# Four node blocks a loop turn on TensorE, VectorE and ScalarE, TensorE's loop bodies cut at another place, and one activation ahead of the first loop

## The chip, the cores and the metric

The kernel runs on one core of one Trainium2 chip. The metric is the device time of one launch in microseconds (us). Times of single instructions are given in us or ns.

## What is computed

100,000 nodes have 64 features each; 50,000 edges, sorted by destination, give `src` and `dst`. Four graph layers follow one another, and each ends in `x = layernorm(x + layer(x))`:

```
L0: three SAGE layers   h = relu(h @ w_self + (segment_sum(h[src], dst) / deg) @ w_neigh + b)
L1: two GCN layers      out = segment_sum(norm * (x @ W)[s], d) + b      (with self loops)
L2: GIN                 x + relu(relu((x + segment_sum(x[src], dst)) @ W1 + b1) @ W2 + b2)
L3: messages            mlp([x[src], x[dst], edge_attr]) summed by dst, then mlp([x, sum])
```

Everything is float32.

## The kernel before

The nodes are padded and cut into 50 blocks (`NB`) of 2,048 nodes, 16 tiles of 128. The program is a chain of passes over all blocks, with a barrier between passes: `Sage0`, `Sage1`, `Sage2`, `Gcn1`, `Gcn2`, `Gin`, `Messages` (empty in this run) and `Update`. Each pass emits a fast version (`windows=True`, the one that runs for sorted edges) and a general one behind a branch on a flag (`both_ways`, L577).

In each pass:

- **GpSimd** gathers the source rows of the block's edges by indirect DMAs of 128 rows into a ring in SBUF, 8 a block (L628), in `Update` 16 a block (L1665). Its loop takes eight blocks a turn.
- **VectorE** builds 0/1 matrices from the edges' destinations (`one_hots`, L649, two for each block), takes the segment sums out of PSUM, and does most of the element work and of the layer norm.
- **TensorE** does the segment sums (`sums`, L659 and L664): for each tile two matrix products of a 0/1 matrix with a ring slot. Which slot that is stands in the table `slots`, so that TensorE's sequencer first loads the slot numbers into registers (`TENSOR_LOAD`, L659) and computes an address ahead of each product. Between sums stand transposes (L968, L1222), first layers (L1208, L1349, L1801 to L1804) and products (L974, L1227). In `Gcn2` there are also matrix products without a use, `stay_warm` (L766).
- **ScalarE** moves results from PSUM to SBUF with an activation, and does squares, roots and part of the norm.
- **SyncE** issues the loads and stores of the blocks. Its loop takes four blocks a turn.

Every engine has its own program; semaphores, which count uses, order them. The loops of TensorE, VectorE and ScalarE are all made by `bodies` (loop at L586): `by=2` blocks a turn in a hardware loop, 24 turns, and the last two blocks unrolled behind it (VectorE and ScalarE in `Update`: 23 turns and four blocks). A turn ends with a compare-and-branch on the engine's sequencer.

Segment sums run one block ahead: in a body for block m, `collect` makes the sums of block m + 1. Where a body of TensorE begins in each pass, before the change:

- `Sage0`: transposes of chunk 0 of block m (four chunks of four tiles), transposes of chunk 1, first layer of chunk 0, sums of chunk 0 of block m + 1, and so on; it ends with the products of chunk 3. Between the transposes of chunks 0 and 1 ScalarE must have emptied the shared PSUM bank (`evacuate`, L1316).
- `Sage2`, `Gcn1`, `Gcn2`: at the segment sums.
- `Sage1`, `Gin`, `Update`: at transposes.

Of the kernel before, what the change touches and what calls it, by code (L numbers as in the profile page):

```python
# [25 lines left out]
ACT = mybir.ActivationFunctionType  # L26
# [34 lines left out]
def build(nc, z, a, out):  # L61
# [512 lines left out]
    def both_ways(eng, general, windows):  # L574
# [4 lines left out]
        with eng.Else():  # L579
            windows()  # L580

    def bodies(eng, body, by=2, behind=2):


        n = (NB - behind) // by
        with eng.Fori(0, n) as it:  # L586
            for v in range(by):
                body(it * by + v, it * (by // 2) + v // 2, v % 2)
        for m in range(n * by, NB):
            body(m, m // 2, m % 2)  # L590
# [12 lines left out]
    def later(m, i, u):  # L603
        return m + 1, i + u, 1 - u
# [165 lines left out]
    class Pass:  # L770
# [133 lines left out]
        def vector_loop(self, ve, windows):  # L904
            for m in range(self.ahead - 1):
                self.hots(ve, m, m, windows)
            self.take_block(ve, 0, 0, 0, windows)
            self.hots(ve, self.ahead - 1, (self.ahead - 1) % 2, windows)
            bodies(ve, lambda m, i, u: self.vector(ve, m, i, u, windows))

        def scalar_loop(self, act, windows):
            bodies(act, lambda m, i, u: self.scalar(act, m, i, u, windows))

        def tensor_loop(self, pe, windows):
            if windows:
                for q in range(2):
                    self.collect(pe, 0, 0, 0, q)
            bodies(pe, lambda m, i, u: self.tensor(pe, m, i, u, windows))

        def gpsimd_windows(self, pool):  # L920
            gather_pool(pool, self.table, self.W, self.pitch, self.last_sum)
# [55 lines left out]
    class Sage2(Pass):  # L977
# [43 lines left out]
                for q in range(2):  # L1021
                    norm_square(act, m + 1, q, pre_of, adds=True)

        def tensor(self, pe, m, i, u, windows):
            if windows:
                for q in range(2):
                    self.collect(pe, *later(m, i, u), q)
            for q in range(2):
                pe.wait_ge(S(f"out{q}"), now(m))
                pe.wait_ge(S(f"ev{q}"), before(m))  # L1030
                pair_transposes(pe, group(store_a[u], q), ps[2 + q]).then_inc(S(f"tr{q}"), 1)
            for q in range(2):
                pe.wait_ge(S(f"ev{q}"), now(m))
                pe.wait_ge(S(f"y{q}"), before(m))
                pair_products(pe, tp[q], wg1, ps[4 + q]).then_inc(S(f"mm{q}"), 1)


    class Gcn1(Pass):
# [33 lines left out]
        def tensor(self, pe, m, i, u, windows):  # L1072
            if windows:
                self.collect(pe, *later(m, i, u), 0)
            for q in range(2):
                pe.wait_ge(S(f"pre{q}"), now(m))
                pe.wait_ge(S(f"ev{q}"), before(m))
                pair_transposes(pe, tmp[1][q], ps[2 + q]).then_inc(S(f"tr{q}"), 1)
            if windows:
                self.collect(pe, *later(m, i, u), 1)  # L1080
            for q in range(2):
                pe.wait_ge(S(f"ev{q}"), now(m))
                pe.wait_ge(S(f"y{q}"), before(m))
                pair_products(pe, tp[q], wg2, ps[4 + q]).then_inc(S(f"mm{q}"), 1)


    class Gcn2(Pass):
# [41 lines left out]
        def scalar(self, act, m, i, u, windows):  # L1129
# [4 lines left out]
            if exists(m + 1):  # L1134
                for q in range(2):
                    norm_square(act, m + 1, q, self.pre(1 - u), True)

        def tensor(self, pe, m, i, u, windows):
            if windows:
                for q in range(2):  # L1140
                    self.collect(pe, *later(m, i, u), q)
                    stay_warm(pe, m * 2 + q, 9)


    class Gin(Pass):
# [107 lines left out]
    class Sage0(Chunks):  # L1253
# [42 lines left out]
        def vector(self, ve, m, i, u, windows):  # L1296
# [7 lines left out]
            for q in range(2):  # L1304
# [2 lines left out]
                own(2 * q + 1)  # L1307
                self.take(ve, *later(m, i, u), q, windows)

        def scalar(self, act, m, i, u, windows):  # L1310
            A = nc.scalar
            self.stored(act, i, u)

            def evacuate(c):
                act.wait_ge(S(f"tr{c}"), now(m))
                A.activation(load_a[u][D:P, c * 512:(c + 1) * 512], ps[4][D:P, :], ACT.Copy).then_inc(S(f"ev{c}"), 1)  # L1316

            def hidden(c):
                act.wait_ge(S(f"hid{c}"), now(m))
                act.wait_ge(S(f"nmm{(c + 2) % 4}"), now(m) if c >= 2 else before(m))  # L1320
                A.activation(tp[c % 2][:, :], ps[5], ACT.Relu, bias=b0c[:, :]).then_inc(S(f"rel{c}"), 1)  # L1321

            def neighbours(c):
                act.wait_ge(S(f"nmm{c}"), now(m))
                A.activation(store_b[u][:, c * 512:(c + 1) * 512], ps[6], ACT.Copy).then_inc(S(f"n1{c}"), 1)  # L1325

            evacuate(0)
            for c in range(4):
                if c < 3:
                    evacuate(c + 1)  # L1330
                hidden(c)
                if c >= 1:
                    neighbours(c - 1)
            neighbours(3)

        def tensor(self, pe, m, i, u, windows):
            def former(name, c):

                pe.wait_ge(S(f"{name}{(c + 3) % 4}"), now(m) if c else before(m))

            def turn(c):
                pe.wait_ge(S(f"mean{c}"), now(m))
# [8 lines left out]
            def products(c):  # L1351
                pe.wait_ge(S(f"rel{c}"), now(m))
                former("n1", c)
                tile_products(pe, tp[c % 2], w1[:, 0:H], ps[6])
                former("s1", c)
                tile_products(pe, tp[c % 2], w1[:, H:2 * H], ps[7]).then_inc(S(f"nmm{c}"), 1)
# [12 lines left out]
            products(0)  # L1369
            next_sums(1)  # L1370
            turn(3)
            hidden(2)
            products(1)
            next_sums(2)
            hidden(3)
            products(2)
            next_sums(3)
            products(3)


    class Sage1(Chunks):
# [210 lines left out]
    class Update(Pass):  # L1592
# [107 lines left out]
        def vector_loop(self, ve, windows):  # L1700
# [9 lines left out]
            bodies(ve, lambda m, i, u: self.vector(ve, m, i, u, windows), behind=4)  # L1710

        def vector(self, ve, m, i, u, windows):
            V = nc.vector
# [49 lines left out]
        def scalar_loop(self, act, windows):  # L1763
# [4 lines left out]
            bodies(act, lambda m, i, u: self.scalar(act, m, i, u, windows), behind=4)  # L1768

        def scalar(self, act, m, i, u, windows):  # L1770
            self.turned(act, "u", 0, m, windows)
# [55 lines left out]
        def tensor_loop(self, pe, windows):  # L1827
            if windows:
# [9 lines left out]
            bodies(pe, lambda m, i, u: self.tensor(pe, m, i, u, windows))  # L1838

        def tensor(self, pe, m, i, u, windows):  # L1840
            both = windows and exists(m + 2)
# [154 lines left out]
```

## Time and profile before

| | |
|---|---|
| time, median of 3 runs | 6260.33 us (6242.03 to 6272.64) |
| profiled execution: span from first to last instruction | 6282.3 us; no other time of that execution is recorded |
| busy share of the span | TensorE 88%, weight loads 79%, VectorE 66%, GpSimd 62%, ScalarE 36% |
| mean granted TensorE clock | 0.897 of full speed |
| pass, us from the span's start | `Sage0` 131 to 1317, `Sage1` 1350 to 2031, `Sage2` 2052 to 2803, `Gcn1` 2833 to 3475, `Gcn2` 3494 to 4147, `Gin` 4182 to 4985, `Update` 5040 to 6282 |

In the profile PE is TensorE's matrix product, PEld its weight load (it overlaps with PE), DVE VectorE, ACT ScalarE, POOL GpSimd, SP SyncE; a q behind the name is the engine's sequencer. Register, branch and semaphore instructions are not counted as busy. PEclk is the granted clock of TensorE, 1.00 being 2.4 GHz and 0.50 being 1.2 GHz; a value between them is the mean over a stretch that has both. An idle time is put down to what released the engine; "issue" means that nothing the profile shows was waited for. A row of windows has, in this order: stretch in us, its length, busy us of PE, PEld, DVE, ACT and POOL with the number of instructions (x), granted clock, share of the DMA engines, GB/s.

### The profile page before, as it was taken

How to read it: one execution, taken by the hardware profiler on the slowest of the kernel's cores; microseconds unless marked ns; L12 is line 12 of the kernel's file. 1: busy time of each engine (PE TensorE's matmuls, PEld its weight loads, DVE VectorE, ACT ScalarE, POOL GpSimd, SP SyncE). 2: the span in 40 equal slices, each digit the busy share in tenths (PEclk: the TensorE clock that was granted, in tenths of full speed). 3: DMA queues.
4: the chain of work that ended last, by engine and by line, in shares of the span. 5: the costliest groups of instructions: out<-in, count | busy, mean ns of one | idle time of the engine just before them, and what ended most of it. 6: DMA issues, size and time to landing. Idle time of an engine off the chain costs nothing. (4 is left out here: it accounts for less than half of the span.)

```text
span 6282.3 us, 130219 instructions
## 1 busy us (share of the span) xinstructions
PE 5525.7 (88%) x39618; PEld 4963.8 (79%) x39619; DVE 4169.7 (66%) x6902; ACT 2249.6 (36%) x6826; POOL 3865.2 (62%) x3226
## 2 busy tenths in 40 slices
PE   3888898969998888978999899969999689999998
PEld 3777777759998788878999899967777567777776
DVE  4444444447776789885666788858888746665655
ACT  0333333322222333330001588843333234444443
POOL 3442442337885666637777677856666377777773
PEclk9999999989999778778888899978888899999998
DMA  1333333335555455543334344432222222222222
GB/s 34 127 121 118 129 112 126 112 123 201 200 201 177 136 161 157 158 142 92 101 101 107 119 141 141 147 80 80 83 85 84 63 58 75 71 71 71 70 72 53
DMA packets 259156, 706.87 MB, mean 113 GB/s; under 512 B 86436, under 2 KB 87620, under 8 KB 236646
## 3 DMA queue, kind: packets, MB, share of 16 engines
q1 hardware_dynamic: 156198, 586.53, 26.5%
q0 software_dynamic: 102848, 119.09, 10.0%
q8 instruction: 43, 0.70, 0.0%
q14 instruction: 67, 0.55, 0.0%
HBM read 389.05 MB, written 314.60 MB: 112 GB/s over the span
## 5 line engine op out<-in xcount | busy, mean ns | idle before, releaser
L664 PE MATMUL ps_all<-arena 128*128 x22400 | 2944.7, 295 | 438.6 <-issue 357.4
L664 PEld LDWEIGHTS ps_all<-arena 128*128 128x128 f32 x22400 | 2871.2, 211 | 548.9 <-issue 543.9
L649 DVE TENSOR_TENSOR arena<-iota,window 128x2048 f32<-128x2048 f32 x708 | 1599.0, 2283 | 30.3 <-issue 24.9
L628 POOL DMA_INDIRECT arena<-n_t,ix_now x800 | 980.4, 1225 | 566.7 <-issue 283.5
L628 POOL DMA_INDIRECT arena<-y_t,ix_now x800 | 996.1, 1245 | 353.9 <-issue 248.3
L628 POOL DMA_INDIRECT arena<-x_rows,ix_now x400 | 453.3, 1133 | 674.1 <-DMA ix_now<-src_ix 413.1
L628 POOL DMA_INDIRECT arena<-x_t,ix_now x400 | 493.5, 1234 | 326.3 <-DMA ix_now<-src_ix 177.1
L1665 POOL DMA_INDIRECT store_a<-x_t,ix_now x400 | 476.5, 1191 | 201.0 <-issue 124.7
L1227 PEld LDWEIGHTS ps_all<-w,tp 128*128 128x128 f32 x4000 | 492.7, 196 | 86.4 <-issue 85.6
L1301 DVE TENSOR_TENSOR store_a<-ps_all,b1r 128x512 f32<-128x512 f32 x200 | 138.3, 692 | 626.3 <-PE ps_all L1227 626.3
L1665 POOL DMA_INDIRECT store_a<-x_t,ix_dst x400 | 450.4, 1126 | 136.8 <-issue 136.5
L1227 PE MATMUL ps_all<-w,tp 128*128 128x128 f32 x4000 | 500.9, 279 | 1.3 <-ACT store_b L1325 0.8
L1403 DVE SCALAR_TENSOR_TENSOR tmp<-ps_all,invdeg,load_a 128x128 f32<-128x128 f32 x800 | 225.2, 344 | 166.5 <-PE ps_all L664 118.5
L1719 DVE TENSOR_TENSOR tmp<-ps_all,bu2r 128x256 f32<-128x256 f32 x200 | 84.9, 425 | 335.5 <-PE ps_all L1227 335.5
L1070 ACT ACTIVATE tp<-ps_all,bg1c 128x512 f32<-128x512 f32 x100 | 65.0, 685 | 595.3 <-PE ps_all L968 594.3
L719 ACT ACTIVATE sq<-tmp 128x64 f32<-128x64 f32 x800 | 191.7, 241 | 229.7 <-DVE tmp L704 229.7
L730 ACT ACTIVATE stat<-stat,eps_c 128x8 f32<-128x8 f32 x400 | 107.7, 293 | 424.3 <-DVE stat L744 424.0
L974 PE MATMUL ps_all<-wg,tp 128*128 128x128 f32 x1600 | 243.0, 315 | 3.4 <-ACT tp L1019 1.1
L1430 ACT ACTIVATE store_b<-ps_all 128x256 f32<-128x256 f32 x200 | 71.7, 384 | 483.4 <-DVE store_a L1416 483.4
L1804 PE MATMUL ps_all<-tp,wu 128*128 128x512 f32 x400 | 213.9, 617 | 33.7 <-ACT tp L1748 33.7
L1227 PEld LDWEIGHTS ps_all<-wu,tq 128*128 128x128 f32 x1600 | 202.5, 192 | 51.7 <-issue 47.8
L1349 PE MATMUL ps_all<-load_a,w 128*128 128x512 f32 x400 | 239.5, 684 | 0.3 <-ACT tp L1321 0.3
(185 smaller groups left out, 7778.5 us busy)
## 6 DMA issues: line engine op xcount, KB each, us to landing
x_t<-store_a SPq DMA_DIRECT2D x150, 512.0 KB, 3.1
load_b<-x_t SPq DMA_DIRECT2D x150, 512.0 KB, 3.3
s_t<-store_a SPq DMA_DIRECT2D x50, 1024.0 KB
n_t<-store_b SPq DMA_DIRECT2D x50, 1024.0 KB
load_a<-s_t SPq DMA_DIRECT2D x50, 1024.0 KB
y_t<-store_b SPq DMA_DIRECT2D x100, 512.0 KB
load_a<-x_cols SPq DMA_DIRECT2D x50, 512.0 KB
s_t<-store_a SPq DMA_DIRECT2D x50, 512.0 KB
```

Source lines behind the costliest of these rows:

```text
L628: pool.indirect_dma_start(out=slot_rows(at, W, pitch), out_offset=None, in_=table, in_offset=bass.IndirectOffsetOnAxis(ap=ix_now[:, at:at ...
L649: V.tensor_tensor(hot_matrices(at, q), iota[:, :].unsqueeze(1).unsqueeze(1).to_broadcast([P, 2, GT, P]), window[:, :, bass.ds(m * NT + q * ...
L664: last = pe.matmul(out(j), hot_matrices(at, j // GT)[:, k, j % GT, :], ring[:, bass.ds(places[k][j - first] * W, W)], start=(k == 0), stop ...
L719: last = A.activation(sq[q][:, j * D:(j + 1) * D], tmp[0][q][:, j * D:(j + 1) * D], ACT.Square, accum_out=stat[:, q, 2, j:j + 1])
L730: nc.scalar.activation(stat[:, q, 3, :], stat[:, q, 2, :], ACT.Sqrt, bias=eps_c[:, :], scale=1.0 / D).then_inc(S(f"sd{q}"), 1)
L974: last = pe.matmul(bank[:, r * P:(r + 1) * P], lhs[:, r * P:(r + 1) * P], w[:, :], start=True, stop=True)
L1227: last = pe.matmul(bank[:, r * P:(r + 1) * P], lhs[:, r * P:(r + 1) * P], w, start=True, stop=True)
L1301: V.tensor_tensor(tiles3(store_a[u][:, c * 512:(c + 1) * 512], H), tiles3(ps[7], H), row(b1r, H, CT), ALU.add).then_inc(S(f"s1{c}"), 1)
L1349: pe.matmul(ps[5], w0[:, :], load_a[u][:, c * 512:(c + 1) * 512], start=True, stop=True).then_inc(S(f"hid{c}"), 1)
L1403: last = nc.vector.scalar_tensor_tensor(tmp[c % 2][q][:, r * P:(r + 1) * P], agg[:, r * P:(r + 1) * P], invdeg[:, bass.ds(m * NT + c * CT ...
L1665: pool.indirect_dma_start(out=self.pairs(u, h)[:, to:to + D], out_offset=None, in_=x3_t, in_offset=bass.IndirectOffsetOnAxis(ap=ix[:, at:a ...
L1804: pe.matmul(ps[4 + s], wu1[:, :], tp[s][:, :], start=True, stop=True).then_inc(S(f"uhid{s}"), 1)
```

## The change

1. `bodies` gets `by=TURN`, four, in the fast version of TensorE, VectorE and ScalarE in all passes: 12 turns and two unrolled blocks in place of 24 and two (VectorE and ScalarE in `Update`: 11 turns and six blocks in place of 23 and four). The general version keeps two.
2. TensorE's body is cut in two: `tensor(m)` is the latter part for block m and then calls `front(m + 1)`, the first part of the next block; one `front(0)` stands ahead of the loop. The order of the instructions on TensorE stays as it was; only where the loop's branch stands in it is new. Bodies now begin: `Sage0` at the products of chunk 3, `Sage2` at the transposes behind both sums, `Gcn1` at the products, `Gcn2` at `stay_warm`. `Sage1`, `Gin` and `Update` have no `front`.
3. `Sage0.scalar_loop` does one Relu on a single element for each partition ahead of the loop.

```diff
+    TURN = 4
-            bodies(ve, lambda m, i, u: self.vector(ve, m, i, u, windows))
+            bodies(ve, lambda m, i, u: self.vector(ve, m, i, u, windows), by=TURN if windows else 2)
-            bodies(act, lambda m, i, u: self.scalar(act, m, i, u, windows))
+            bodies(act, lambda m, i, u: self.scalar(act, m, i, u, windows), by=TURN if windows else 2)
+        def front(self, pe, m, i, u, windows):
+            pass
-            bodies(pe, lambda m, i, u: self.tensor(pe, m, i, u, windows))
+            self.front(pe, 0, 0, 0, windows)
+            bodies(pe, lambda m, i, u: self.tensor(pe, m, i, u, windows), by=TURN if windows else 2)
 # Sage2
-        def tensor(self, pe, m, i, u, windows):
+        def front(self, pe, m, i, u, windows):
             if windows:
                 for q in range(2):
                     self.collect(pe, *later(m, i, u), q)
+
+        def tensor(self, pe, m, i, u, windows):
...
+            self.front(pe, *later(m, i, u), windows)
 # Gcn2
+        def front(self, pe, m, i, u, windows):
+            if windows:
+                self.collect(pe, *later(m, i, u), 0)
+
         def tensor(self, pe, m, i, u, windows):
             if windows:
-                for q in range(2):
-                    self.collect(pe, *later(m, i, u), q)
-                    stay_warm(pe, m * 2 + q, 9)
+                stay_warm(pe, m * 2, 9)
+                self.collect(pe, *later(m, i, u), 1)
+                stay_warm(pe, m * 2 + 1, 9)
+            self.front(pe, *later(m, i, u), windows)
 # Sage0
+        def scalar_loop(self, act, windows):
+
+            nc.scalar.activation(stat[:, 1, 4, 0:1], eps_c[:, :], ACT.Relu)
+            super().scalar_loop(act, windows)
...
         def tensor(self, pe, m, i, u, windows):
+            self.products(pe, m, 3)
+            self.front(pe, *later(m, i, u), windows)
```

`Sage0.front` holds what `Sage0.tensor` held, without the products of chunk 3; `Gcn1.front` holds sums, transposes and sums, and `Gcn1.tensor` the products and the next `front`. `Update`, which has loops of its own, gets the same `by`.

## Rows read from the trace of the kernel before

**Rows 1.** The page's first part: busy us, share of the span, instructions.

```profile
PE 5525.7 (88%) x39618; PEld 4963.8 (79%) x39619; DVE 4169.7 (66%) x6902; ACT 2249.6 (36%) x6826; POOL 3865.2 (62%) x3226
```

**Rows 2.** Busy time by windows, one for each of six passes.

```profile
131.00:1317.00 1186.00, 1057.95 (x7536) 911.60 (x7536) 518.86 (x1085) 404.27 (x622) 433.95 (x381) 0.94 0.37 119
1350.00:2031.00 681.00, 652.53 (x5600) 635.90 (x5600) 508.08 (x1099) 172.04 (x400) 516.75 (x400) 0.98 0.57 191
2052.00:2803.00 751.00, 672.85 (x4376) 644.77 (x4376) 660.55 (x992) 270.76 (x1777) 453.98 (x393) 0.78 0.50 152
2833.00:3475.00 642.00, 596.85 (x4400) 591.61 (x4400) 401.76 (x398) 64.95 (x100) 485.81 (x393) 0.83 0.35 101
4182.00:4985.00 803.00, 722.13 (x4600) 611.15 (x4600) 668.41 (x998) 278.92 (x500) 483.87 (x392) 0.86 0.27 80
5040.00:6282.00 1242.00, 1160.37 (x7568) 925.91 (x7568) 718.90 (x1194) 493.24 (x896) 897.96 (x773) 0.98 0.24 67
```

**Rows 3.** Waits of POOL in the passes Gcn1 and Update.

```profile
POOL arena L628 <- issue: 118.6, 368, 4.2
...
POOL store_a L1665 <- issue: 253.2, 764, 3.5
```

**Rows 4.** One line's instructions: ScalarE's L1316, whole span.

```profile
L1316 ACT ACT_TABLE_LOAD  x24: 1283/1283/1283, 101.8 to 1232.9; - x24
```

**Rows 5.** Timeline of ACT and PE around the end of a turn of Sage0.

```profile
1138.29 1.28 ACT L1316 ACT_TABLE_LOAD   x1
...
1140.32 0.63 PE L1222 MATMUL ps_all<-ident,load_b 128*128 128x128 f32 x4 [2.25 <-ACT load_a L1316]
...
1143.18 1.99 PE L664 MATMUL ps_all<-arena 128*128 x16 [1.38 <-issue]
...
1162.48 0.63 PE L1222 MATMUL ps_all<-ident,load_b 128*128 128x128 f32 x4 [0.96 <-ACT load_a L1316]
```

**Rows 6.** Windows from block to block of Sage0, columns as in rows 2.

```profile
1140.30:1162.50 22.20, 19.85 (x153) 17.40 (x153) 9.46 (x19) 7.51 (x12) 2.84 (x4) 1.00 0.32 108
1162.50:1187.50 25.00, 21.48 (x153) 18.45 (x153) 11.61 (x27) 8.79 (x13) 0.00 (x0) 0.93 0.33 122
...
1235.20:1260.90 25.70, 24.43 (x153) 20.66 (x152) 9.43 (x18) 7.51 (x12) 0.00 (x0) 0.80 0.23 78
```

**Rows 7.** Windows of two turns of Sage2, columns as in rows 2.

```profile
2157.50:2184.20 26.70, 21.54 (x179) 20.02 (x178) 26.70 (x41) 10.94 (x72) 21.21 (x19) 1.00 0.58 179
2184.20:2216.10 31.90, 29.01 (x178) 27.80 (x178) 26.78 (x41) 11.01 (x72) 17.25 (x17) 0.73 0.46 148
```

**Rows 8.** Timeline of PE in Sage2: segment sums that open a turn.

```profile
2160.83 7.46 PE L664 MATMUL ps_all<-arena 128*128 x64 [1.96 <-issue]
...
2307.84 11.52 PE L664 MATMUL ps_all<-arena 128*128 x64 [2.07 <-issue]
```

**Rows 9.** Sequencer instructions of three lines: ns minimum/median/maximum.

```profile
L586 PEldq COMPARE_BRANCH  x168: 76/208/250, 179.8 to 6224.7; - x168
...
L659 PEldq TENSOR_LOAD <-slots x1800: 328/588/1862, 118.3 to 6233.4; - x180
...
L577 PEldq COMPARE_BRANCH  x9: 235/438/3658, 94.0 to 4995.8; - x9
```

**Rows 10.** The chain of work in Update: a sum in each block.

```profile
5100.48 3.78 PE ps_all L664 x32
5124.14 3.78 PE ps_all L664 x32
...
5148.32 3.78 PE ps_all L664 x32
```

**Rows 11.** A whole turn of Sage0, by windows, columns as in rows 2.

```profile
1135.50:1182.70 47.20, 41.35 (x307) 35.85 (x306) 21.07 (x45) 16.30 (x25) 7.03 (x6) 0.96 0.34 118
```

**Rows 12.** DMA queues from 300 to 1200 us: every queue that moved a packet.

```profile
q1 hardware_dynamic: 15416, 99.72, 31.7%
q0 software_dynamic: 9312, 9.55, 5.2%
```

More of the change, by code:

```diff
@@ L1070, in scalar @@
                 nc.scalar.activation(tp[q][:, :], ps[2 + q], ACT.Relu, bias=bg1c[:, :]).then_inc(S(f"ev{q}"), 1)
-        def tensor(self, pe, m, i, u, windows):
+        def front(self, pe, m, i, u, windows):
+            if not exists(m):
+                return
             if windows:
@@ L1080, in tensor @@
                 self.collect(pe, *later(m, i, u), 1)
+        def tensor(self, pe, m, i, u, windows):
             for q in range(2):
@@ L1136, in scalar, with front @@
                     norm_square(act, m + 1, q, self.pre(1 - u), True)
+        def front(self, pe, m, i, u, windows):
+            if windows:
+                self.collect(pe, *later(m, i, u), 0)
         def tensor(self, pe, m, i, u, windows):
             if windows:
-                for q in range(2):
-                    self.collect(pe, *later(m, i, u), q)
-                    stay_warm(pe, m * 2 + q, 9)
+                stay_warm(pe, m * 2, 9)
+                self.collect(pe, *later(m, i, u), 1)
+                stay_warm(pe, m * 2 + 1, 9)
+            self.front(pe, *later(m, i, u), windows)
     class Gin(Pass):
@@ L1334, in scalar, with products, former, front @@
             neighbours(3)
-        def tensor(self, pe, m, i, u, windows):
+        def products(self, pe, m, c):
+            def former(name):
+                pe.wait_ge(S(f"{name}{(c + 3) % 4}"), now(m) if c else before(m))
+            pe.wait_ge(S(f"rel{c}"), now(m))
+            former("n1")
+            tile_products(pe, tp[c % 2], w1[:, 0:H], ps[6])
+            former("s1")
+            tile_products(pe, tp[c % 2], w1[:, H:2 * H], ps[7]).then_inc(S(f"nmm{c}"), 1)
+        def tensor(self, pe, m, i, u, windows):
+            self.products(pe, m, 3)
+            self.front(pe, *later(m, i, u), windows)
+        def front(self, pe, m, i, u, windows):
+            if not exists(m):
+                return
             def former(name, c):
@@ L1349, in hidden @@
                 pe.matmul(ps[5], w0[:, :], load_a[u][:, c * 512:(c + 1) * 512], start=True, stop=True).then_inc(S(f"hid{c}"), 1)
[L1351 to L1356, printed above, removed]
             def next_sums(c):
@@ L1368, in tensor @@
             hidden(1)
-            products(0)
+            self.products(pe, m, 0)
             next_sums(1)
@@ L1372, in tensor @@
             hidden(2)
-            products(1)
+            self.products(pe, m, 1)
             next_sums(2)
             hidden(3)
-            products(2)
+            self.products(pe, m, 2)
             next_sums(3)
-            products(3)
     class Sage1(Chunks):
@@ L1709, in vector_loop @@
             self.messages(ve, 0, windows)
-            bodies(ve, lambda m, i, u: self.vector(ve, m, i, u, windows), behind=4)
+            bodies(ve, lambda m, i, u: self.vector(ve, m, i, u, windows), by=TURN if windows else 2, behind=4)
         def vector(self, ve, m, i, u, windows):
@@ L1767, in scalar_loop @@
             self.message_units(act, 0, windows)
-            bodies(act, lambda m, i, u: self.scalar(act, m, i, u, windows), behind=4)
+            bodies(act, lambda m, i, u: self.scalar(act, m, i, u, windows), by=TURN if windows else 2, behind=4)
         def scalar(self, act, m, i, u, windows):
@@ L1837, in tensor_loop @@
                     self.collect(pe, 0, 0, 0, q)
-            bodies(pe, lambda m, i, u: self.tensor(pe, m, i, u, windows))
+            bodies(pe, lambda m, i, u: self.tensor(pe, m, i, u, windows), by=TURN if windows else 2)
         def tensor(self, pe, m, i, u, windows):
```

## The prediction

> **What bounds the kernel now.** I read the busy shares first [rows 1]: TensorE is busy in 88% of the span, no other engine in more than 66%. Since the passes are parted by barriers, the share says little; the windows by pass say which engine sets the pace in each [rows 2].
>
> `Sage0`: TensorE (1058 of 1186 us), GpSimd far from it. `Sage1`: TensorE is busy 652.5 of 681 us at a clock of 0.98, so there is almost no idle time for a better loop to win. `Sage2`: VectorE is busy 660.6 of 751 us and TensorE 672.9, but at a clock of 0.78; the two take turns. `Gcn1`: TensorE works at 0.83 and GpSimd is the bound: 485.8 us of gathers plus 118.6 us of idle time, 0.32 us ahead of each, is 604 of 642 us [rows 2, 3]. `Gcn2` is alike. `Gin`: TensorE 722 of 803 us at 0.86. `Update`: the chain of waits runs mostly over TensorE [rows 10], with GpSimd just beneath: 898.0 + 253.2 = 1151 of 1242 us [rows 2, 3].
>
> So there are two kinds of time that a change of TensorE's loops can reach: idle time at a turn's end, and the half-speed clock that follows idle time.
>
> **The table load of `Sage0`.** ScalarE has 24 table loads of 1.283 us, one in each turn, all on the first activation of the loop body [rows 4]; ScalarE's work needs none, since the other blocks do the same activations without one. TensorE waits for that activation: 2.25 us at the turn's end, against 0.96 us in the block between two ends [rows 5]. The difference of 1.29 us is the load, and nothing covers it. The first load, at 101.8 us, lies ahead of the first gather and stays in another form: the new Relu brings it, at the same place. The new Relu makes the table's state known ahead of the loop, so I take it that the 23 others go: 23 x 1.29 = 30 us. Were the load to stay in the loop, twelve turns in place of 24 would still give half, 15 us.
>
> The Trainium skill (ScalarE: Activation LUTs, What ACT_TABLE_LOAD costs) gives the load 1283 ns, and another 1380 ns for a drain, for each switch to another set. The trace agrees on the first and shows no second part in TensorE's wait; by the page the sum would be 23 x 2.66 = 61 us.
>
> **The clock in `Sage0`.** A block that holds no table load and no slow stretch takes 22.2 us; one with a table load and a clock of 0.93 takes 25.0, so that 25.0 - 22.2 - 1.3 = 1.5 us are the clock's; a block whose clock is 0.80 takes 25.7, which is 3.5 us for the clock [rows 6]. The pass's mean is 1186 / 50 = 23.7 us a block, so the clock costs 23.7 - 22.2 - 0.6 (half a table load) = 0.9 us a block, some 45 us in all. A clock falls behind both kinds of idle time: the one with the table load, and the shorter pair, 0.96 us and then some 1.4 us for the slot numbers ahead of the sums [rows 5, 6]. The longer idle time goes, the shorter pair stays in each block. If every block then had a slow stretch at 1.5 us, that is 50 x 1.5 = 75 us, 30 worse than now, and the table's gain is gone; if none had, 45 us are won. The rows decide for neither; the nearest is that the cost remains as it is, and I take 0, bounds -45 and +30.
>
> **The turn's end itself.** On TensorE's sequencer the branch takes 0.208 us [rows 9], and two register instructions beside it some 0.08 more, about 0.29 us. VectorE's and ScalarE's branches I cost at nothing: both wait for TensorE around them in the passes that TensorE sets, and if that cover were gone, as in a `Sage2` that VectorE bounds, they would be below the 0.29 us of TensorE's. Where TensorE's body begins at the sums, these 0.29 us stand in a row with the slot loads (0.588 us each, up to 1.862 [rows 9]) between the last product and the first sum. That row of steps is 1.96 to 2.07 us of idle time in `Sage2` [rows 8]. Behind the change the branch stands behind 64 sum products, where the sequencer is ahead, and the gap is 0.29 us shorter. The slot loads are not moved against the products: their stall stays, in every block.
>
> Directly that is 24 x 0.29 = 7 us at most. But a turn without a slow stretch takes 26.7 us, with VectorE busy in all of them, and one with it 31.9 at a clock of 0.73; the same 64 sum products take 7.46 and 11.52 us [rows 7, 8]. All 50 blocks at 13.35 us would be 668 us, 83 less than now. Half of the turn ends go and the others are hidden, so fewer slow stretches should begin; but idle times of 1.7 us remain, and 1.96 us was harmless once while 2.07 was not. Bounds: 0 and 83. I take a quarter, 20 us, nearer to the nothing that an idle time only a seventh shorter suggests.
>
> **`Gcn1`, `Gcn2`, `Sage1`.** In the first two GpSimd's gathers set the pace; a faster turn only makes TensorE wait longer for rows. Only what follows the last gather could gain. `Sage1`'s end lies beneath products. I take 0, bounds 0 and 15 us for the tails.
>
> **`Gin`, `Update`.** Their bodies begin where they did; 12 turn ends fewer are 12 x 0.29 = 3.5 us in `Gin`, taken as 4, with its slow stretches (clock 0.86) as they are. In `Update` the same sum in neighbouring blocks is 23.66 and then 24.18 us apart [rows 10]: 0.52 us for a turn's end, so 12 x 0.52 = 6 us, if GpSimd allows it (it has 91 us of slack).
>
> **The sum.** 30 + 0 + 20 + 0 + 4 + 6 = 60 us, from 6282.3 us to 6222.3 us for the profiled execution. Its span lies 22 us above the median of the runs; against the median: 6260 - 60 = 6200 us.
>
> **The rivals.**
>
> *The clock takes the gain back.* TensorE gets faster by little, and waits at the same places. In `Sage0` the pair of idle times that stays meets a slow stretch in every block (+30), so nothing of 30 is left; `Sage2` keeps its pattern. For it: the block of 25.0 us at 0.93 begins behind the shorter pair [rows 5, 6]. Against it: the longest slow stretch, at 0.80, follows the table load. Left are 4 + 6 us: 6250 us.
>
> *The clock stays up.* `Sage0` wins 30 + 45 us, `Sage2` 50 of its 83, `Gin` and the tails 15, with 6 in `Update`: 146 us, so 6114 us. For it: the turn at 26.7 us exists [rows 7]. Against it: it is rare, and the slot loads stay.
>
> *Slower: a turn of four blocks no longer fits where the sequencer keeps its code.* Now it fits: in 900 us of `Sage0` no packet moved on any queue but the two for data [rows 12], and the branch at L586 never took over 0.250 us. A turn of `Sage0` has 307 + 306 products and weight loads [rows 11] and the sequencer's own on top; four blocks double it, more than any loop of the trace shows. Where a target is not at hand, the trace has the price: the branch at L577 took up to 3.658 us, against 0.235 [rows 9], so 3.4 us. In the two longest loops, `Sage0` and `Update`, with 12 turns each, and with a slow stretch of 3.5 us behind each such stop [rows 6], that is 24 x 6.9 = 166 us; with the 60 won, 6260 + 106 = 6366 us. It decides as soon as a turn is larger than the store; against it stands only that nothing near the limit shows at half the size.
>
> The Trainium skill (Runtime: NRT & Kernel Launch, Instruction fetch mechanics) says that a taken branch whose target lies outside the pages held forces a fetch, and that TensorE holds 2,048 instructions, the other engines 512. By that size a turn of four would fit and this rival would fall; by its remark that a store is only two lines it could bite. No run here shows the limit.
>
> *The change does only part of what it says*: the table load stays in the loop. Then 15 + 20 + 10 = 45 less 10 for more slow stretches: 6225 us.
>
> **How the numbers follow.** Forecast 0.49, the clock takes it back 0.22, the clock stays up 0.18, slower 0.07, table load stays 0.04. Half a per cent is 31 us and about what a measurement of this kernel can tell from no change, so the bound for faster is 6229 us. The forecast falls below it nine times in ten, the clock staying up always, the remaining table load half the time, the second case rarely: 0.49 x 0.9 + 0.18 + 0.02 + 0.03 = 0.67. Slower is the code rival and a little: 0.08. The rest, 0.25, is no change. The range goes from the case of the clock staying up, 6110, to a little above the case in which it takes all back, 6270. The forecast's own range is 6165 to 6235.
>
> **What would show it.** Right: one table load on ScalarE in all of `Sage0`, or none in its loop; TensorE's wait for L1316 at 0.96 us in every block; 84 branches at L586 on TensorE in place of 168; idle time before the sums of `Sage2` at 1.7 us and its clock above 0.78; `Gcn1` and `Gcn2` as long as they were, GpSimd's gathers unbroken; sums in `Update` 23.7 us apart in three of four blocks. Wrong: table loads in each turn; branches at L586 of over 3 us, or instruction packets in the middle of a pass; a clock in `Sage0` below 0.94 with blocks of 23.7 us or more; `Gcn1` shorter by more than 15 us, which would mean that GpSimd was not its bound. The prediction fails upward if slow stretches simply settle elsewhere, and downward if they vanish.

## The result, and the profile after

The changed kernel takes 6173.82 us (median of 4 runs, 6155.04 to 6188.64), the kernel before 6263.97 (4 runs). The ratio is 0.9871, with a 95% interval from 0.9839 to 0.9902. Forecast were 6200 us, 60 less than before; it became 90 less by the medians, and 110 in the profiled executions, from 6282.3 to 6172.2 us of span. Some 20 of those 110 come from the profiled execution of the kernel before, whose span alone lies 18 us above that kernel's median. The mean granted clock rose from 0.897 to 0.914.

The page's first part, as [rows 1]:

```profile
PE 5428.5 (88%) x39618; PEld 4877.7 (79%) x39619; DVE 4168.7 (68%) x6902; ACT 2218.5 (36%) x6804; POOL 3886.7 (63%) x3226
```

TensorE's instructions are the same in number, and it is busy for 97 us less: that is the clock. ScalarE has 22 instructions fewer: 23 table loads are gone and the new Relu has come. The one load left in `Sage0` stands at 101.4 us, on that Relu.

The windows that follow go from the branch that opens a pass to the next one, so that none of a pass's time is left out (those of [rows 2] begin and end inside the pass). Columns: PE, PEld, DVE, ACT and POOL busy, clock, DMA share, GB/s. The kernel before, in the order `Sage0`, `Sage1`, `Sage2`, `Gcn1`, `Gcn2`, `Gin`, and `Update` last:

```profile
101.00:1342.00 1241.00, 1071.10 (x7600) 924.57 (x7600) 542.27 (x1109) 408.31 (x626) 453.34 (x400) 0.93 0.36 117
...
2036.00:2817.00 781.00, 678.43 (x4400) 649.83 (x4400) 672.64 (x1002) 274.78 (x1800) 463.60 (x400) 0.77 0.49 152
...
4163.00:4989.00 826.00, 722.13 (x4600) 611.15 (x4600) 677.30 (x1002) 278.92 (x500) 493.54 (x400) 0.85 0.27 80
```

The changed kernel, the same windows:

```profile
101.00:1288.00 1187.00, 1034.48 (x7600) 898.60 (x7600) 542.50 (x1109) 378.99 (x604) 456.27 (x400) 0.96 0.38 122
1288.00:1979.00 691.00, 646.34 (x5600) 632.03 (x5600) 512.34 (x1100) 170.78 (x400) 513.57 (x400) 0.98 0.58 190
1979.00:2728.00 749.00, 639.51 (x4400) 608.30 (x4400) 673.15 (x1003) 274.42 (x1800) 477.90 (x400) 0.82 0.51 158
2728.00:3382.00 654.00, 589.60 (x4400) 585.20 (x4400) 410.82 (x402) 64.83 (x100) 493.48 (x400) 0.83 0.35 101
3382.00:4072.00 690.00, 615.25 (x5000) 607.22 (x5000) 566.77 (x902) 554.85 (x2500) 509.76 (x400) 0.90 0.43 134
4072.00:4882.00 810.00, 709.13 (x4600) 599.76 (x4600) 677.05 (x1002) 280.06 (x500) 495.85 (x400) 0.86 0.28 81
...
4889.00:6172.00 1283.00, 1169.12 (x7600) 929.88 (x7600) 730.33 (x1202) 494.52 (x900) 925.06 (x800) 0.96 0.24 67
```

`Sage0` is 54 us shorter, `Sage2` 32 and `Gin` 16. The four others (694, 659, 687 and 1286 us before, in the same windows) moved by 5 us or less.

What TensorE waited for in `Sage0` (total us, times, longest), first before, then after:

```profile
PE ps_all L1222 <- ACT load_a L1316: 77.4, 50, 2.2
PE ps_all L664 <- issue: 49.4, 42, 1.4
```

```profile
PE ps_all L666 <- issue: 61.3, 48, 1.4
PE ps_all L1241 <- ACT load_a L1340: 47.7, 50, 1.0
```

The wait for the activation is 29.7 us shorter: 50 waits of at most 1.0 us, where 24 had been 2.2. The wait ahead of the segment sums, which no engine ends ("issue"), grew by 11.9 us. TensorE's busy time fell by 36.6, with the clock up from 0.93 to 0.96. The three make the 54 us: 29.7 - 11.9 + 36.6 = 54.4.

TensorE in a block of `Sage0` after, to be held against [rows 5]:

```profile
1136.34 0.63 PE L1241 MATMUL ps_all<-ident,load_b 128*128 128x128 f32 x4 [0.96 <-ACT load_a L1340]
1136.80 1.02 PE L1391 MATMUL ps_all<-load_a,w 128*128 128x512 f32 x2
1139.03 1.99 PE L666 MATMUL ps_all<-arena 128*128 x16 [1.20 <-issue]
...
1158.33 0.63 PE L1241 MATMUL ps_all<-ident,load_b 128*128 128x128 f32 x4 [0.96 <-ACT load_a L1340]
```

The 2.25 us at a turn's end are gone; the pair of 0.96 us and some 1.2 us for the slot numbers stands in every block. The block takes 22.0 us.

The loop's instructions on TensorE's sequencer (ns minimum/median/maximum), as in [rows 9]:

```profile
L588 PEldq COMPARE_BRANCH  x84: 76/208/247, 240.1 to 6118.5; - x84
...
L661 PEldq TENSOR_LOAD <-slots x1800: 325/588/2137, 118.1 to 6127.6; - x180
```

Half the branches, none longer than before: a turn of four fits. The queues from 300 to 1000 us in the middle of `Sage0`, as in [rows 12], move no instructions:

```profile
q1 hardware_dynamic: 12272, 79.30, 32.7%
q0 software_dynamic: 7939, 8.15, 5.8%
```

### The profile page after: what moved, and what is told of

The parts are those of the page before. It is cut to its first block and busy times, and to the rows that moved or that the text cites. A ratio compares the mean times of both kernels' runs of the same rounds, so it can differ in the third digit from the quotient of the medians.

```text
span 6172.2 us, 129380 instructions
## 1 busy us (share of the span) xinstructions
PE 5428.5 (88%) x39618; PEld 4877.7 (79%) x39619; DVE 4168.7 (68%) x6902; ACT 2218.5 (36%) x6804; POOL 3886.7 (63%) x3226
## 5 line engine op out<-in xcount | busy, mean ns | idle before, releaser
L666 PE MATMUL ps_all<-arena 128*128 x22400 | 2877.2, 291 | 439.2 <-issue 357.8
L666 PEld LDWEIGHTS ps_all<-arena 128*128 128x128 f32 x22400 | 2806.0, 207 | 538.9 <-issue 533.1
L1699 POOL DMA_INDIRECT store_a<-x_t,ix_now x400 | 461.4, 1153 | 201.7 <-issue 124.7
L1699 POOL DMA_INDIRECT store_a<-x_t,ix_dst x400 | 463.7, 1159 | 137.2 <-issue 136.6
L1838 PE MATMUL ps_all<-tp,wu 128*128 128x512 f32 x400 | 212.9, 614 | 29.0 <-ACT tp L1782 29.0
L980 PEld LDWEIGHTS ps_all<-wg,tp 128*128 128x128 f32 x1600 | 223.4, 223 | 16.8 <-ACT tp L1025 16.2
```

Of the source, the lines that this page charges most:

```text
L666: last = pe.matmul(out(j), hot_matrices(at, j // GT)[:, k, j % GT, :], ring[:, bass.ds(places[k][j - first] * W, W)], start=(k == 0), stop ...
L980: last = pe.matmul(bank[:, r * P:(r + 1) * P], lhs[:, r * P:(r + 1) * P], w[:, :], start=True, stop=True)
L1699: pool.indirect_dma_start(out=self.pairs(u, h)[:, to:to + D], out_offset=None, in_=x3_t, in_offset=bass.IndirectOffsetOnAxis(ap=ix[:, at:a ...
L1838: pe.matmul(ps[4 + s], wu1[:, :], tp[s][:, :], start=True, stop=True).then_inc(S(f"uhid{s}"), 1)
```

## The experiments

### The change taken apart

Four kernels on one chip: the Relu alone, all without the Relu, the cut alone, and four blocks a turn alone.

```diff
 e1_table_only: the kernel before, and in Sage0
+        def scalar_loop(self, act, windows):
+            nc.scalar.activation(stat[:, 1, 4, 0:1], eps_c[:, :], ACT.Relu)
+            super().scalar_loop(act, windows)
 e2_all_but_table: the changed kernel without these three lines
 e3_cut_only: e2 with
-    TURN = 4
+    TURN = 2
 e4_four_only: the kernel before with TURN = 4, and in each of the three loops of Pass and of Update
-            bodies(pe, lambda m, i, u: self.tensor(pe, m, i, u, windows))
+            bodies(pe, lambda m, i, u: self.tensor(pe, m, i, u, windows), by=TURN if windows else 2)
```

> The kernel before with the Relu ahead of Sage0's loop and nothing else. If the table load costs only its own time, the 23 loads in the loop go, TensorE's wait for the evacuation is 0.96 us in every block, and Sage0 is 30 us shorter, the other passes as before: 0.995 of the kernel before. If removing the long idle time also spares slow clock, as the changed kernel's Sage0 suggests (54 us shorter in the profile), Sage0 is 45 to 55 us shorter with half the low-clock time: 0.991 to 0.993. If the clock settles elsewhere, Sage0 is about as long as before.

> The changed kernel without the Relu: one table load a turn, so 12 in Sage0's loop. Theory 1 (the load and the clock behind it): Sage0 wins about half, 25 us against the kernel before, the other passes as in the changed kernel, 0.991 to 0.993 of the kernel before. Rival (the gain in Sage0 comes from fewer turn ends and the cut, not from the table): Sage0 is as short as in the changed kernel, near 1187 us from its branch to the next pass's.

> Bodies cut as in the changed kernel, still two blocks a turn, no Relu. If hiding the branch behind work is what helps Sage2, its 2.0 us of idle time ahead of the sums at a turn's end become 1.7, its low-clock time falls from 361 us and the pass is 15 to 35 us shorter; Gin and Update, which are not cut, stay as before; 0.995 to 0.998 in all. If the number of turn ends is what counts, Sage2 stays at 781 us.

> Four blocks a turn, bodies not cut, no Relu. 12 table loads fewer give 15 us in Sage0 (25 with the clock). If the number of turn ends counts in Sage2, half of its slow stretches go: 15 to 35 us; Gin 4 to 16 us shorter, Update 3 to 6; in all 0.990 to 0.995. If the cut is what helps Sage2, that pass stays near 781 us and the whole is at 0.994 to 0.997.

| kernel | median us | ratio to before, 95% | `Sage0` | `Sage2` | `Gin` |
|---|---|---|---|---|---|
| before | 6255.61 | | 1241 | 781 | 826 |
| e1_table_only | 6207.08 | 0.9932 (0.9908 to 0.9957) | 1195 | 777 | 813 |
| e2_all_but_table | 6191.65 | 0.9891 (0.9852 to 0.9930) | 1212 | 760 | 804 |
| e3_cut_only | 6231.47 | 0.9963 (0.9941 to 0.9985) | 1241 | 744 | 825 |
| e4_four_only | 6208.21 | 0.9921 (0.9897 to 0.9945) | 1215 | 755 | 806 |

(The passes are those of each kernel's profiled execution, in us; the median of the kernel before is that of its 21 runs beside these.) `Sage0` in e1, e3 and e4, by windows:

```profile
101.00:1296.00 1195.00, 1041.10 (x7600) 902.97 (x7600) 542.04 (x1109) 378.87 (x604) 452.75 (x400) 0.96 0.38 121
```

```profile
101.00:1342.00 1241.00, 1072.44 (x7600) 925.14 (x7600) 542.22 (x1109) 408.17 (x626) 450.66 (x400) 0.93 0.36 117
```

```profile
101.00:1316.00 1215.00, 1055.41 (x7600) 913.21 (x7600) 542.39 (x1109) 392.91 (x614) 452.06 (x400) 0.94 0.37 119
```

The Relu alone takes 46 us off `Sage0`, not 30. TensorE's wait for the activation falls by the 29.7 us again (77.4 to 47.7), and its busy time by 30.0, 1071.1 to 1041.1: the clock is up from 0.93 to 0.96 with nothing else of this pass changed. With twelve of the 24 loads left, e4 has half of both: the wait is 61.9 us, busy time 15.7 less. The cut alone, which leaves the 24 loads, changes nothing in `Sage0`. So each table load in the loop cost 1.29 us of wait and about as much again in half-speed products behind it. Of the 60 us that both come to for all 23 loads, the wait for the slot numbers takes back some 14. Of the two theories put down ahead of e1 the second held (45 to 55 us were forecast, 46 came). e2, which differs from the changed kernel by the Relu alone, has 12 loads in place of one and takes 1212 us: the rival that fewer turn ends made `Sage0` shorter forecast 1187 and is out.

In `Sage2` both halves of the change work, and don't add: the cut gives 37 us, four blocks a turn 26, the two together 32 in the changed kernel and 21 in e2, which has the same `Sage2`. Two executions of one code thus lie 11 us apart, and the order of the four is not shown; that each is shorter than the 781 and 777 of the uncut loop with two blocks is. In `Gin`, whose code the Relu and the cut don't touch, the three kernels with two blocks took 826, 813 and 825 us; with four a turn it took 810, 804, 806, and 806 and 799 in e6 and e7 below. That is about 16 us for four blocks a turn, with up to 13 us between two executions of the same code.

### How large may a turn be

```diff
-    TURN = 4
+    TURN = 8
```

> The changed kernel with eight blocks a turn (the unrolled rest grows to two blocks on TensorE, ten in Update on VectorE and ScalarE). A turn on TensorE is then some 1,800 to 2,000 sequencer instructions in Sage2, Gcn1, Gcn2 and Gin, some 2,300 in Sage1 and some 3,000 in Sage0 and Update. If there is a limit to the code that is held and it lies between, branches at the loop's line take some 3.5 us in the passes above it, instruction packets move in the middle of these passes, Sage0 and Update are 6 x 7 = 40 us longer each, and the passes below the limit are as in the changed kernel or 5 us shorter: 1.00 of the kernel before. If code streams in ahead of the sequencer at no cost, nothing stops and the whole is at 0.985 to 0.988 of the kernel before, as the changed kernel or a little faster.

Measured: 6292.48 us, ratio 1.0053 (1.0030 to 1.0076). The sequencer's branch, whole span:

```profile
L588 PEldq COMPARE_BRANCH  x42: 76/3652/6967, 333.1 to 6219.4; - x42
```

The median of all branches is 3.652 us in place of 0.208, and in the middle of `Sage0` two more queues now move packets:

```profile
q8 instruction: 51, 0.84, 0.5%
q14 instruction: 20, 0.16, 0.1%
```

Each pass now has five stops. By windows `Sage0` is 20 us longer than with four blocks a turn, `Sage1` 17, `Sage2` 14, `Gin` 33 and `Update` 32; `Gcn1` and `Gcn2` are not longer. For `Sage0` and `Update` 40 each had been forecast. The slower rival was a true mechanism, and four blocks stayed below its edge. To find the edge, six blocks a turn, in one run:

```diff
-    TURN = 4
+    TURN = 6
```

> The changed kernel with six blocks a turn: some 2,200 sequencer instructions in a turn of TensorE in Sage0 and Update, 1,700 in Sage1, 1,350 to 1,480 in the four others. If what is held lies between the 1,490 of the changed kernel's Sage0 and 1,700, the branch takes some 3.5 us in Sage0, Sage1 and Update and 0.2 us elsewhere; if it lies between 1,700 and 2,200, Sage1 is free of it too. If four blocks were already near the edge and other things than size decide, the four shorter passes stop as well.

Measured: 6239.44 us. The branch in `Sage0`, in `Sage1`, in the four passes behind it, and in `Update`:

```profile
L588 PEldq COMPARE_BRANCH  x8: 83/5202/5597, 289.6 to 1285.6; - x8
...
L588 PEldq COMPARE_BRANCH  x8: 76/208/234, 1438.5 to 1987.3; - x8
...
L588 PEldq COMPARE_BRANCH  x32: 76/208/228, 2144.4 to 4883.7; - x32
...
L588 PEldq COMPARE_BRANCH  x8: 76/3332/3777, 5142.9 to 6180.1; - x8
```

Only the two longest bodies stop. From branch to branch the trace records, with the sequencer's own instructions, some 2,213 on TensorE in a turn of six blocks of `Sage0` and 1,705 in one of `Sage1`, which runs on without a stop. At eight blocks a turn of `Sage2` or `Gcn1` has some 1,791, and every branch back stops, for 3.472 and 3.824 us in the median. So the edge lies between 1,705 and 1,791 recorded instructions, and a turn of four in `Sage0`, 1,477, is 13% below the longest turn that ran free. (A trace can lack some records, so that the true numbers may be a little higher.) The price: `Sage0` took 1228 us, 41 more than at four, with seven stops of 5.2 us, and `Update` 1310, 27 more, with seven of 3.3. A stop thus cost 4 to 6 us in all, of which the branch itself is 3.3 to 5.2. The prediction's 6.9 us a stop was too high.

The Trainium skill (Runtime: NRT & Kernel Launch, Instruction fetch mechanics) puts TensorE's store at 2,048 instructions. The runs confirm that a branch back stops the engine once the loop is too long, and that instructions are then fetched in the middle of a pass. They don't show a loop that makes full use of the 2,048. Its remark on two lines, which the prediction weighed, did not bite: the loop of 1,705 ran free.

### Is it the clock, or the wait behind the products

Two theories of what was left in `Sage2` at 749 us, where VectorE's work is 673: the half-speed clock holds TensorE back, or the wait for the slot numbers does, by where it stands. Two kernels from the changed one. The first adds work that computes nothing, nine small products ahead of the sums of each block, to keep TensorE busy. Each is two on TensorE, so that the pass has 900 more:

```diff
 e6_warm_sage2, Sage2.tensor
+            if windows:
+                stay_warm(pe, m, 9)
             self.front(pe, *later(m, i, u), windows)
```

The second reads the slot numbers of the first half's sums at the body's start, ahead of the transposes, and not behind the products. No load is added or taken away (1800 in either kernel):

```diff
 e7_slots_ahead_sage2
+    def places_of(m, tiles):
+        first, n = tiles[0], len(tiles)
+        return [nc.values_load_multi_w_load_instructions(slots[0:1, k, bass.ds(m * NT + first, n)], ...)[1] for k in range(2)]
-    def sums(pe, m, tiles, out, W, at):
+    def sums(pe, m, tiles, out, W, at, places=None):
+        places = places or places_of(m, tiles)
...
         def tensor(self, pe, m, i, u, windows):
+            places = places_of(m + 2, range(GT)) if windows and exists(m + 2) else None
...
-            self.front(pe, *later(m, i, u), windows)
+            self.front(pe, *later(m, i, u), windows, places)
```

> The changed kernel with nine products without a use ahead of the segment sums of each block of Sage2 (2.0 us more work for TensorE a block, 100 us in the pass). They give the sequencer time to load the slot numbers, so that no idle time stands ahead of the sums. If the low clock that follows this idle time is what makes Sage2 longer than VectorE's 13.35 us a block, the pass gets shorter in spite of the added work: from 749 us to 700 to 720, with less than 120 us of low clock (now 274). If TensorE's amount of work is what counts, the pass grows, by up to 50 us. Other passes as in the changed kernel.

> The changed kernel; in Sage2 the slot numbers of the first half of a block's sums are loaded at the beginning of the body, ahead of the transposes, and no longer between products and sums. The idle time ahead of the sums should vanish (1.7 us), and since VectorE takes 13.35 us a block in any case, it moves ahead of the transposes. If any idle time of that size lowers the clock, the pass stays at 740 to 750 us with 270 us of low clock. If it is the place ahead of the sums that matters, because the 64 sum products then run at the low clock while the transposes' idle time is harmless, the pass falls to 700 to 725 us.

`Sage2` by windows, in e6 and in e7:

```profile
1977.00:2711.00 734.00, 672.53 (x5300) 647.00 (x5300) 673.15 (x1002) 272.34 (x1800) 482.65 (x400) 0.91 0.52 161
```

```profile
1977.00:2684.00 707.00, 595.36 (x4400) 571.12 (x4400) 671.79 (x1002) 274.88 (x1800) 485.76 (x400) 0.85 0.55 167
```

e6 lifted the clock from 0.82 to 0.91 and won 15 us of the pass, less than was expected of it (700 to 720 us, and under 120 us of low clock, where a mean of 0.91 over 734 us makes some 130); the kernel's median, 6171.94, cannot be told from the changed kernel's. The added products take 109 us, and TensorE's own work in the pass fell from 640 to 564 (672.5 - 108.7), so the better clock was paid for with more than it gave. e7 lifted the clock only to 0.85 and won 42 us: 6127.65 us, ratio 0.9796 (0.9762 to 0.9831). TensorE's waits in the whole pass, after the change and then in e7:

```profile
PE ps_all L666 <- issue: 63.0, 34, 25.0
PE ps_all L974 <- DVE store_a L760: 42.8, 37, 8.2
```

```profile
PE ps_all L979 <- DVE store_a L765: 84.6, 48, 6.8
PE ps_all L671 <- issue: 25.3, 2, 25.0
```

25 us of "issue" in either are the pass's first wait. The rest of it, 38 us in 33 waits, is gone, but the waits for VectorE grew by 42: TensorE idles as long as before, some 110 us. What fell is its busy time, 639.5 to 595.4 us, and that is the pass's 42 us. The sums alone (busy us of PE and PEld, then clock, DMA share and GB/s), after the change and in e7:

```profile
1979.00:2728.00 749.00, 444.30 (x3200) 437.31 (x3200) 0.82 0.51 158
```

```profile
1977.00:2684.00 707.00, 378.26 (x3200) 377.76 (x3200) 0.85 0.55 167
```

They lost 66 us of busy time, while the transposes and products ahead of them gained 28. So the half-speed clock was the cost, and the place of the idle time decides what runs at it: ahead of the sums it was the 64 sum products of a block, ahead of the transposes it is mostly the few products behind these. That is the second theory put down for e7 (700 to 725 us), but for its word "harmless". Now TensorE waits for VectorE in nearly every block, and VectorE sets the pace, busy 672 of 707 us.

### The same in `Sage0` and `Gin`

e8 does this in three passes: in `Gin` both halves' slot numbers ahead of the transposes, in `Sage0` those of chunk 0 ahead of the last products.

```diff
 e8_slots_ahead_three: e7, and
 Sage0
         def tensor(self, pe, m, i, u, windows):
+            places = places_of(m + 2, range(CT)) if windows and exists(m + 2) else None
             self.products(pe, m, 3)
-            self.front(pe, *later(m, i, u), windows)
+            self.front(pe, *later(m, i, u), windows, places)
...
 Gin
         def tensor(self, pe, m, i, u, windows):
+            places = [places_of(m + 1, range(q * GT, q * GT + GT)) if windows and exists(m + 1) else None for q in range(2)]
...
-                    self.collect(pe, *later(m, i, u), q)
+                    self.collect(pe, *later(m, i, u), q, places[q])
```

> The changed kernel with slot numbers loaded at the beginning of the body in three passes: Sage2 as in the run before (707 us), Gin (both halves of the sums, ahead of the transposes) and Sage0 (chunk 0 of the next block, ahead of the products of chunk 3). If the idle time ahead of the sums and the clock behind it are the cost there too, Sage0 falls from 1187 to 1110 to 1135 us (1.3 us a block and its 88 us of low clock), Gin from 806 to 730 to 780, and the whole is at 0.960 to 0.970 of the kernel before. If Gin and Sage0 wait for other things anyway (VectorE's input to the transposes, ScalarE's evacuation), the idle time moves there and the whole is at 0.977 to 0.981.

Measured: 5934.96 us (4 runs, 5931.63 to 5952.33), ratio 0.9502 (0.9479 to 0.9525). It beats both kernels, lies 239 us below the changed one, and below the range that was forecast for it (0.960 to 0.970): `Sage0`, 1080 us where 1110 to 1135 were expected, makes about half of that. `Sage0`, `Sage2` and `Gin` by windows:

```profile
101.00:1181.00 1080.00, 988.77 (x7600) 880.49 (x7600) 542.00 (x1109) 379.00 (x604) 473.88 (x400) 0.99 0.42 134
...
1864.00:2571.00 707.00, 595.93 (x4400) 571.69 (x4400) 671.82 (x1002) 274.93 (x1800) 485.11 (x400) 0.85 0.54 167
...
3905.00:4637.00 732.00, 633.50 (x4600) 543.30 (x4600) 675.20 (x1002) 277.46 (x500) 505.57 (x400) 0.94 0.31 90
```

`Sage0` lost 107 us more. A stretch of it, with the same instructions as shown above of the changed kernel:

```profile
608.73 0.63 PE L1248 MATMUL ps_all<-ident,load_b 128*128 128x128 f32 x4 [0.96 <-ACT load_a L1347]
609.20 1.02 PE L1399 MATMUL ps_all<-load_a,w 128*128 128x512 f32 x2
610.06 1.90 PE L671 MATMUL ps_all<-arena 128*128 x16
...
629.26 0.63 PE L1248 MATMUL ps_all<-ident,load_b 128*128 128x128 f32 x4 [0.96 <-ACT load_a L1347]
```

No idle time ahead of the sums; the block takes 20.5 us. The 61.3 us of waits are gone, and 45.7 us of busy time with them. Most of that is the clock, now 0.99. Some 12 us are not: in blocks at full clock TensorE is busy for 19.83 us after the change and for 19.54 to 19.61 in e8, as its products follow each other without a break. The wait for the activation alone, 0.96 us, stays in each of the 50 blocks and does little to the clock. The pair did.

In `Gin`, as in `Sage2`, the idle time moves. Its waits (us, times, longest), after the change and in e8:

```profile
PE ps_all L666 <- issue: 95.6, 89, 39.4
PE ps_all L974 <- DVE load_a L1175: 10.5, 27, 1.0
```

```profile
PE ps_all L979 <- DVE load_a L1181: 49.0, 40, 1.5
PE ps_all L671 <- issue: 39.3, 1, 39.3
PE ps_all L979 <- issue: 9.9, 9, 1.5
PE ps_all L1234 <- ACT tp L1206: 4.8, 20, 0.3
```

TensorE idles about as long as before (106 us and 103), in fewer waits (116 and 70). The timeline shows where, first after the change, ahead of either half's sums, then in e8, ahead of the transposes alone:

```profile
4316.50 3.78 PE L666 MATMUL ps_all<-arena 128*128 x32 [0.77 <-issue]
4320.88 5.12 PE L666 MATMUL ps_all<-arena 128*128 x32 [0.59 <-issue]
```

```profile
4315.09 1.25 PE L979 MATMUL ps_all<-ident,load_a 128*128 128x128 f32 x8 [0.99 <-DVE load_a L1181]
...
4320.22 7.26 PE L671 MATMUL ps_all<-arena 128*128 x64
```

The clock is 0.94 in place of 0.86, and busy time falls from 709 to 634 us, which is nearly all of the pass's 78 us. Some 15 of these 76 are not the clock: at full clock the 64 sum products take 7.26 us in one run and twice 3.78 in two.

Last, whether the larger turn is still worth having with the slot numbers ahead:

```diff
 e10_slots_two_a_turn: e8 with
-    TURN = 4
+    TURN = 2
```

> The kernel of the run before last (slot numbers loaded early in Sage0, Sage2 and Gin, bodies cut, Relu ahead) with two blocks a turn in place of four. If the number of turn ends has a cost of its own, the 12 turns more cost 3 to 16 us in Gin and 3 to 6 in Update, and the whole is at 0.952 to 0.956 of the kernel before. If turn ends only mattered through the idle time that they lengthened, ahead of slot loads that are now hidden, the three passes are within 5 us of those with four blocks a turn, and the whole is at 0.949 to 0.952.

Measured: 5974.75 us, ratio 0.9552 (0.9529 to 0.9574), 40 us above e8. In `Sage0` and `Sage2` nothing is lost (1079 and 707 us). `Gin` takes 752 us in place of 732, `Gcn1` 658 in place of 650, `Sage1` 691 in place of 683. Of the two theories neither holds for all: with the slot numbers ahead a turn's end is free in `Sage0` and `Sage2`, and `Gin` is 20 us longer, more than the 3 to 16 of the first theory. The 40 us of the medians are clear of the noise, but by passes only `Gin`'s 20 us are more than executions of one code lie apart: `Gcn1` took 658 to 661 us in the four kernels with two blocks a turn and 650 to 661 in those with four, `Sage1` 688 to 694 and 683 to 691. `Update`, for which the first theory forecast 3 to 6 us, took 1285 and 1288.

## Why the prediction was right, and where its sizes were off

- *The table load.* Right in place and size: 29.7 us of TensorE's wait against 30 in the sum, and 23 loads gone. Nothing of a second part beside the 1.283 us is seen in TensorE's wait: it fell by 29.7 us in e1, too, not by the 61 that come of the figures of the Trainium skill (ScalarE: Activation LUTs, What ACT_TABLE_LOAD costs). What a load cost beyond that is TensorE's clock.
- *The clock in `Sage0`*, "the nearest is that the cost remains as it is, and I take 0". This step was mis-sized: the busy time fell by 36.6 us, the slot waits grew by 11.9, so the term is -24 (the bounds were -45 and +30). The prediction read two kinds of idle time, and weighed the shorter pair against the longer wait by the slow stretches of two blocks. By e1 and e4 the longer one's share follows the number of table loads: 23 fewer gave 30.0 us of busy time, 12 fewer 15.7. The rival that the clock takes the gain back falls with it.
- *`Sage2`.* 32 us in place of 20, within its bounds. "0.29 us shorter" was too small: gaps of 1.61 to 1.86 us stood in some blocks still, but without the pass's first wait the idle time ahead of the sums fell from 51 us to 38, and the clock went from 0.77 to 0.82. Busy time fell by 39 us and those waits by 13, and the waits for VectorE took 18 of it back. The term was mis-sized, and why either half of the change alone does about as much as both stays open.
- *`Gin`.* 16 us in place of 4, mostly the clock again (busy time 13 us less); up to 13 us of such a difference is seen between two executions of the same code, so that this size is uncertain; the kernels taken apart give the same 16.
- *`Update`.* 6 us forecast, and this step failed: the pass went from 1286 to 1283 us, and with the same body in turns of two it took 1280 us in e1 and e3. TensorE's wait for ScalarE (L1804, later L1838) did fall, from 33.7 us to 29.0, as in every kernel with four blocks a turn (28.9 to 29.1; 33.7 or 33.8 with two). But GpSimd covers it. The prediction's 91 us of slack were not slack: 85 of them are the pass's tail behind the last gather, at 6197.7 us. Up to there GpSimd is busy or in the 0.33 us ahead of a gather. The kernel before (columns as in [rows 2]), and GpSimd's waits in the pass after the change:

```profile
5040.00:6197.00 1157.00, 1097.70 (x7233) 875.83 (x7233) 678.01 (x1114) 465.99 (x847) 897.25 (x773) 0.99 0.25 69
```

```profile
POOL store_a L1699 <- issue: 261.2, 790, 3.8
```

897 us busy and the 253 us of such waits [rows 3] are 1150 of these 1157 us. The 800 gathers, from first to last, take 1194.8 us before and 1194.7 after, 23.9 us a block. The prediction's 0.52 us between 23.66 and 24.18 us [rows 10] were thus not shown to be a turn's end that would go: the two average to GpSimd's pace. No run here makes GpSimd faster, so that this reading rests on the traces alone.
- *`Gcn1`, `Gcn2`, `Sage1`.* 0 forecast; 5 us less, 3 more, 3 less, within what executions of one code differ by. GpSimd was the bound of the first two, as read, and the trace has it so in `Sage1`, too: its 400 gathers take 651 us from first to last before and 650 after.
- *The larger turn's size.* Right that it fits; the rival's mechanism is real, and begins between 1,705 and 1,791 recorded instructions.
- *"The slot loads are not moved against the products: their stall stays, in every block."* True of nearly every block of `Sage0`, and the largest cost that these runs took out. The prediction used it only as a reason why the clock would stay down. Moving the loads gave 239 us (6173.82 to 5934.96, in sets of runs whose medians of the kernel before differ by 12), where the whole change gave 90.

The sum came out as 110 us against 60 in the profiled executions: 30 for the table load as forecast, 24 for `Sage0`'s clock in place of 0, 32 for `Sage2` in place of 20, 16 for `Gin` in place of 4, and 3 to 5 for each of the rest, of both signs. The mechanisms of the first four were those of the prediction; three of their sizes were too small, and the median came out 26 us below the forecast.

## What to carry to other kernels

Where a page gives TensorE idle time "issue" ahead of products whose addresses come from registers, look for the loads of these registers on its sequencer, and move them to where the engine has queued work: the same loads in another place gave 4% here. Price a stall that recurs in a loop twice, once for its length and once for the half-speed stretch behind it, look which idle times stand close together, and ask which products run behind them. Where another engine holds the pace, idle time can't be removed, but moved ahead of less work. Before a bound's idle time is called slack, look whether it lies inside the loop or behind its last instruction. When a loop body grows, count its instructions on the sequencer against the size at which a branch begins to cost microseconds.

## What the runs showed of the hardware that was not expected

- A turn's branch on TensorE goes from 0.208 us to 3.3 to 5.3 us (medians of passes, e5 and e9) between 1,705 and 1,791 recorded instructions in the loop, below the 2,048 that the Trainium skill gives for the store (Runtime: NRT & Kernel Launch, Instruction fetch mechanics).
- A pass with as much idle time can have a much better clock: `Gin` with 106 us of waits in 116 pieces at 0.86, and with 103 us in 70 at 0.94 (e8), when the waits stood mostly in one place of each block, ahead of the transposes.
- A single idle time of 0.96 us in each block left the clock at 0.99 in `Sage0` (e8), a pair of 0.96 and 1.2 at 0.96.
- A load of slot numbers takes 0.588 us in the median, but up to 2.137 us in the changed kernel. The Trainium skill (DMA: Bandwidth & Descriptors, Latency and other measured facts) gives a `tensor_load` a floor of about 600 ns; the shortest here took 0.325 us.
